# Position maxima taken in front of the turning of the projected tile, in the first attention phase

## The reference

```python
x = x + attn_a(layernorm(x))   # 32 heads of 16, 8 key/value heads, rotary positions, causal softmax
x = x + ffn(layernorm(x))      # 512 -> 1376 -> 512, 4-bit codes with scales plus a rank-32 correction
x = x + attn_b(layernorm(x))   # 32 heads of 16, biases, causal softmax
x = x + ffn(layernorm(x))
```

## Time and profile before

| | us |
|---|---|
| median of 3 runs | 1864.1 |
| lowest, highest | 1847.99, 1868.69 |
| the profiled execution, device time | 1864.23 |
| its span in the trace | 1862.1 |

### The profile page before, as it was taken

How to read it: one execution, slowest core, us unless ns; L and a number is a source line. 1 busy time by engine, 2 the same in 40 slices (tenths; PEclk the granted TensorE clock), 3 DMA queues, 4 the chain that set the end, 5 groups by cost and what they waited for, 6 DMA issues and landing times. The chain is left out here.

```text
span 1862.1 us, 31544 instructions
## 1 busy us (share of the span) xinstructions
PE 1663.4 (89%) x10736; PEld 1159.2 (62%) x10736; DVE 1098.9 (59%) x2401; ACT 862.2 (46%) x1537; POOL 594.1 (32%) x1542
## 2 busy tenths in 40 slices
PE   5888989989987999999678899889899878999997
PEld 4555655655645777877555566566466456777785
DVE  6777677676663845545455655655654638464543
ACT  4556555555552545435334443443444435454441
POOL 3445344444340312213124333333433312131211
PEclk9999999999997999999889899999899899999999
DMA  2000100100114410112333533433453335201010
GB/s 103 2 25 14 36 24 13 36 25 14 36 36 137 152 68 1 68 38 70 110 51 47 80 59 69 75 54 69 69 70 64 52 112 179 79 23 68 0 45 23
DMA packets 78117, 106.95 MB, mean 57 GB/s; under 512 B 13194, under 2 KB 49674, under 8 KB 77972
## 3 DMA queue, kind: packets, MB, share of 16 engines
q1 hardware_dynamic: 77972, 105.10, 23.4%
HBM read 62.34 MB, written 16.78 MB: 42 GB/s over the span
## 5 line engine op out<-in xcount | busy, mean ns | idle before, releaser
L1495 POOL TENSOR_TENSOR f_ht<-f_work,f_ht 128x512 fp32r<-128x512 f32 (+1 forms) x88 | 114.5, 1305 | 513.6 <-ACT f_ht L1553 513.6
L921 ACT ACTIVATE aa_region<-aa_scores 128x512 f32<-128x512 f32 x320 | 184.7, 599 | 84.0 <-PE aa_scores L1215 80.9
L921 ACT ACTIVATE ab_region<-ab_scores 128x512 f32<-128x512 f32 x320 | 181.2, 601 | 73.4 <-PE ab_scores L1215 72.8
L1638 DVE TENSOR_TENSOR f_work<-f_ring,f_work 128x512 f32<-128x512 f32 (+1 forms) x176 | 120.4, 689 | 133.9 <-ACT f_work L1542 111.8
L1542 ACT ACTIVATE f_work<-f_ring,f_scales 128x512 f32<-128x512 f32 (+1 forms) x176 | 120.3, 685 | 165.8 <-PE f_ring L295 165.4
L295 PE MATMUL f_ring<-xt,f_up_codes 128*128 128x512 f32 (+1 forms) x704 | 180.1, 398 | 8.9 <-DVE f_work L1638 4.5
L295 PE MATMUL f_ring<-f_dcodes,f_ht 128*128 128x512 f32 (+1 forms) x704 | 174.5, 402 | 9.9 <-DVE f_down_x L1607 9.4
L295 PE MATMUL f_ring<-xt,f_gate_codes 128*128 128x512 f32 (+1 forms) x704 | 181.7, 401 | 0.0
L774 POOL TENSOR_SCALAR_AFFINE_SELECT ab_region<-ab_region 128x256 f32<-128x256 f32 (+1 forms) x320 | 115.1, 366 | 182.7 <-ACT ab_region L921 182.1
L1175 PE MATMUL ab_maxima<-ab_stacks 96*128 96x128 bf16 (+3 forms) x512 | 143.7, 318 | 25.1 <-DMA ab_stacks<-ab_parted 13.6
L1175 PE MATMUL aa_maxima<-aa_stacks 96*128 96x128 bf16 (+3 forms) x512 | 142.9, 313 | 25.5 <-DVE aa_nmax L1035 17.7
(11 more groups left out here) (190 smaller groups left out, 3067.2 us busy)
## 6 DMA issues: line engine op xcount, KB each, us to landing
ab_stacks<-ab_parted SPq DMA_DIRECT2D x192, 128.0 KB, 4.2
f_raw<-mid SPq DMA_DIRECT2D x32, 256.0 KB, 4.5
f_x<-mid SPq DMA_DIRECT2D x28, 256.0 KB, 4.2
f_raw<-in_gate_q SPq DMA_DIRECT2D x10, 512.0 KB, 5.4
f_raw<-in_up_q SPq DMA_DIRECT2D x10, 512.0 KB, 4.2
f_raw<-in_down_q SPq DMA_DIRECT2D x10, 512.0 KB, 3.9
aa_x<-in_x SPq DMA_DIRECT2D x18, 256.0 KB, 2.9
ab_x<-mid SPq DMA_DIRECT2D x18, 256.0 KB, 3.1
```

Source lines behind the costliest of these rows:

```text
L921: act.activation(probs[:, s // 2 % 2, SUB * (s % 2) + i, :], scores[:, sbk, :], ACT.Exp, scale=0.25).then_inc(scores_freed[sbk].sem, 1)
L1495: pool.tensor_tensor(ht[0:r, LO, n, :], hid[0:r, n % 2, :], ht[0:r, HI, n, :].bitcast(F32), ALU.subtract).then_inc(hid_lo.sem, 1)
L1638: dve.tensor_tensor(dst, src, scaled[0:r, j, :], ALU.add)\
```

## The change

In VectorE's list the call of `maxima_of` for the position moves from behind the loop over the P tasks to in front of it. Nothing is added or removed, no buffer or semaphore changes, and no other engine's stream is touched.

```diff
                         dve.tensor_tensor(rest[:], src, parted[:, a, 0, :], ALU.subtract)\
                            .then_inc(banks.is_free(where, (kind, u, 0, 0)), 1)
+                    if step is not None:
+                        maxima_of(region, b, s, i)
                     for _, bb, u, t in table.started(region, pos, 1, "P"):
 
                         dve.wait_ge(v_hi.sem, v_hi.at(b0 + bb, u * NT + t + 1))
...
                             rotate(where, b0 + bb, u, t)
                         else:
                             remainder(where, b0 + bb, u, t)
-                    if step is not None:
-                        maxima_of(region, b, s, i)
                     tokens_of(region, pos, b0)
                     if rope:
                         for _, bb, u, t in table.started(region, pos, 2, "P"):
```

## The result

The changed kernel took 1870.72 us as the median of 19 runs, the kernel before 1861.61 us over 19; the ratio is 1.0047 with a 95% interval of 1.0034 to 1.006. That is 8.7 us (6.3 to 11.2) slower; 9.2 us were forecast (1873.4, counted from 1864.2). A second series of the same kernel gave 1.0047 again.

A forecast was written before the change was run, and what follows sets the result against it. TensorE was taken to bound the kernel, busy 89% of the span. Place terms, 4 x (0.27 + 0.51 + 0.27 + 0.34) + 3 x (0.27 + 0.40 + 0.27 + 0.27) = 9.2 us, took 1864.2 to 1873.4; range 1858 to 1885.

The forecast's parts named there:

- Can the idle time be filled?: VectorE's wait before the rotation: no, the maxima block completes 0.24 us after the rotation could start, 0.03 with block 2.
- What moves: Block 0 or 1: rotation, task bank and `roped` 0.81 us later, maxima buffer 1.19 earlier, VectorE's work behind 0.27 later.
- P at 9: Projection at position 9, four places: late bank delays the second T part, then the next; +0.51 us each, the worst.
- P at 49: Projection at position 49, three places: as at 9, but two VectorE waits swallow the bank's delay; +0.40 us each.
- P at 4: Projection at position 4, four places: bank costs nothing, VectorE's unbroken run before block 5 starts later; +0.27 us each.
- I leave it out of the sum: Late `roped` holds ScalarE's copy and one exponential; up to 0.1 us more at P at 9, elsewhere under other waits.
- P at 15: Projection at position 15, four places: the T part's delay disappears in the next wait, for VectorE's F finish; +0.27 us each.
- P at 21: Projection at position 21, block 2, four places: T part 0.53 us later, block 5's 0.19 wait goes; +0.34 each.
- The sum: All 28 places: 5.6 + 3.6 = 9.2 us slower, 1873.4 us, +0.5%.
- P at 55: Projection at position 55, three places: as at 15, with a 0.2 us wait on block 5; +0.27 us each.
- The clock: New stops bring 1.2 GHz stretches at some of 8 places, 1.41 us per fall; at most 1884.7 us; chance 0.12.
- Buffers come free earlier, and that wins: Rival: TensorE's waits on maxima shrink at 28 places, -15.1 us, 1849.1 us, faster by 0.8%; chance 0.05.

The follow-up runs named there:

- the two kernels with the idle instruction: Kernel before plus one unread VectorE sum of constant tiles at 28 places, in front of the rotation (ratio 1.007) or behind its sum (1.0075).
- block 2 alone: Kernel before with the maxima moved in front of the rotation only at the four places with maxima block 2; ratio 1.000.
- late bank: Kernel before, but at 24 places the task bank is freed by the first reduction behind the rotation, 0.72 us later; ratio 0.9993.
- statistics first: Kernel before, with the statistics of a coming x tile taken in front of the rotation behind P at 44, three places; ratio 0.9957.

## Why the prediction was right, point by point

- **Can the idle time be filled? No.** Right. The block is complete 0.24 to 0.27 us behind the v copy at the places with block 0 or 1. The kernel in which TensorE makes it earlier gets back four fifths of the loss in the distances 9 to 15, 15 to 21 and 55 to 60, but only a third of it in 60 to 4 and half in 4 to 9.
- **What moves.** Right: the T part that takes the bank starts 2.16 us after the projection's end instead of 1.36, 0.80 later (forecast 0.81), the list 0.27. That the list is paid one for one was argued; the two kernels with the idle instruction show it (0.41 us at 28 places, 13 and 14 us).
- **P at 9, +0.51: too much, measured 0.28.** The step that failed is the readiness of the next T part. It was taken as its start less the idle time of its row, 188.67 - 0.30. The idle time counts from the modelled end of the matmul in front; the rows show the next one starting before such an end (190.38 behind 190.27 + 0.27). In the profile after the T part follows its predecessor by 192.48 - 191.29 = 1.19 us without a wait, not 1.35. With 1.19 the walk gives 187.83 + 1.19 = 189.02, +0.35, and the part does start 0.34 us later (3.35 us behind the projection's end, 3.01 before). Behind P at 49 the same reading made 0.40 of 0.21. The late bank is even less than that: alone it costs some 0.1.
- **P at 4, 15, 21 and 55: too little, by 0.10 to 0.20.** Three steps failed. The first is "I leave it out of the sum", of `roped`. Behind P at 4 it is the chain over ScalarE, which the forecast set to nothing: the remainder L1020 waits for the high part, and that for the sum.

```profile
182.44 0.32 DVE L1001 TENSOR_TENSOR aa_turned<-aa_tasks,aa_trig 128x160 f32<-128x160 f32 x1
...
184.01 0.46 ACT L931 CAST aa_staged<-aa_rest 128x320 bf16<-128x320 f32 x1 [1.29 <-DVE aa_rest L1007]
...
184.50 0.49 DVE L1020 TENSOR_TENSOR aa_rest<-aa_rest,aa_staged 128x320 f32<-128x320 f32 x1
...
185.02 0.39 PE L1215 MATMUL aa_scores<-aa_stacks 99*128 99x256 bf16 x2 [1.06 <-ACT aa_region L921]
```

  It runs 184.50 - 182.44 = 2.06 us after the rotation's start, at once behind ScalarE's copy (184.01 + 0.46), and VectorE, which would have been ready 0.1 us before, lost that. Also, TensorE here waits 1.06 us for the exponential held behind that copy; it lies under the wait that follows, as forecast. The second was not seen at all: behind P at 15 and 55 the sum itself became 0.10 us longer, as a mask of GpSimd was still running when it started (last section).

  The third is the 0.19 us that the forecast gives back behind P at 21, "and that goes": it was the wait of a weight load, and the product behind it hardly gained. The changed kernel (the projection ends at 214.30), and below it the one row of the kernel before (210.16) that the earlier trace rows does not show:

```profile
216.59 0.65 PE L1328 MATMUL aa_tasks<-identb,aa_staged 128*96 128x128 bf16 x8 [0.69 <-DVE aa_turned L1003]
...
217.58 0.38 PE L1175 MATMUL aa_maxima<-aa_stacks 96*128 96x512 bf16 x1
```

```profile
212.92 0.39 PE L1175 MATMUL aa_maxima<-aa_stacks 96*128 96x512 bf16 x1
```

  The T part waits 0.69 us for the bank instead of 0.16 and starts 0.52 later, counted from the projection's end; block 5 stands at 3.28 instead of 2.76, still 0.52 later. So here it is the late bank that TensorE pays, some 0.5 us at each of four places, while VectorE's list loses next to nothing. Two other kernels show the same distance 21 to 44: the one with the change at block 2 alone has 38.74 us, and the one of the last section, whose sums are not lengthened, 38.69 and 38.74.
- **The sum.** 9.2 forecast, 8.7 measured, 9.8 by the distances. Measured less forecast, -0.9 us for P at 9 and -0.6 for P at 49 stand against +0.4 for each of P at 4 and 15, +0.8 for P at 21 and +0.3 for P at 55. That they nearly cancel is luck; the total is better than its terms. As the rows now have it, 24 x 0.27 of list, 4 x 0.5 of the bank behind P at 21, 4 x 0.1 of the chain behind P at 4 and 0.6 of lengthened sums are 9.5 us.
- **The clock.** Partly right as a mechanism, and no part of the sum. One of the signs by which the prediction would be wrong did appear: the projection of P at 9 ran at half clock in three of four batches, where before it did in none:

```profile
455.63 0.39 PE L1215 MATMUL aa_scores<-aa_stacks 99*128 99x256 bf16 x2 [1.06 <-ACT aa_region L921]
...
457.13 0.39 PE L1175 MATMUL aa_maxima<-aa_stacks 96*128 96x512 bf16 x1 [0.83 <-DVE aa_nmax L1035]
...
457.39 3.89 PE L295 MATMUL aa_tasks<-aa_w,xt 128*128 128x384 f32 x12
```

  The projection took 3.89 us instead of 2.35, behind waits of 1.06 and 0.83 us where there was one of 1.28. These falls belong to the change: 4 to 9 holds one in 8 of 12 batches of the two profiles of the changed kernel and of the one with late masks, and in 1 of 16 of the four kernels whose order at this place is the old one (before, late bank, block 2 alone, statistics first). The Trainium skill's rule that activity releases the full clock (TensorE: Matmul & The Clock Gate, What's actually happening) fits these rows. But the same profile has lost two stretches in which the kernel before fell (60 to 4 took 33.96 and 33.94 us there and 31.01 here), so the first matmul of the feed-forward ring starts at 583.0 us in the changed kernel's profile and at 584.1 in that before. The second profile of the changed kernel falls at 4 to 9 in two batches and not in three. Over the runs the two sides about cancel: the mean granted clock was 0.955 in the 10 and 19 runs of the changed kernel and 0.954 in the 24 of the kernel before, so the slowdown is not lost clock. Such falls come and go by 1.4 us and more, and hide a change of 9 us in a single profile.
- **Buffers come free earlier, and that wins.** Did not happen: TensorE's idle time in front of the maxima products fell from 23.6 us to 19.0 (a fall of over 5 was named as a sign of being wrong), but those in front of T parts (+6.4), scores (+4.6) and F (+2.3) grew by more. Only kernels that shorten VectorE's list or fill its waits won.

## What to carry to other kernels

When an engine works through a fixed list, ask of a move what its list behind the moved part loses or gains, before asking what is released earlier: here 0.27 us of list at 24 places, 6.5 us, was most of the cost, and a bank released 0.7 us late at those places cost almost nothing. At the other four, where TensorE was already waiting for the bank, its delay of 0.5 us was paid in full. So look too for the places where the waiting engine already waits for what the move makes later. Before moving work into an engine's idle time, compare to a tenth of a microsecond when that work's input is complete; work that needs nothing of the awaited producer (the statistics) is what fits there. A saving of the order of 0.5% on this kernel is read from distances between recurring events in the trace, at equal clock, and not from a profile's span.

## What the runs showed that was not expected

**VectorE and GpSimd hold each other.** VectorE's sum of 128x320 takes 0.49 us alone and longer when a mask of GpSimd is still running as it starts. The timeline of the changed kernel behind P at 15:

```profile
204.55 0.41 POOL L774 TENSOR_SCALAR_AFFINE_SELECT aa_region<-aa_region 128x256 f32<-128x256 f32 x1 [0.66 <-ACT aa_region L921]
204.71 0.59 DVE L1007 TENSOR_TENSOR aa_rest<-aa_turned 128x320 f32<-128x320 f32 x1
```

The 7 sums behind P at 15 and 55 took 0.59 us and the 4 behind P at 21 0.66, with a mask of 256 columns ending 0.25 and 0.32 us into them (as above, 204.55 + 0.41 - 204.71); behind P at 9, where it ends 0.14 us in, the sum took 0.49. In the kernel before only one of 28 took over 0.52. It works the other way too: the mask of 128 columns, 0.29 us alone, took 0.44 where it began 0.20 us into a sum, in the kernel before:

```profile
179.58 0.49 DVE L1007 TENSOR_TENSOR aa_rest<-aa_turned 128x320 f32<-128x320 f32 x1
179.78 0.44 POOL L774 TENSOR_SCALAR_AFFINE_SELECT aa_region<-aa_region 128x128 f32<-128x128 f32 x1 [0.21 <-ACT aa_region L921]
```

The Trainium skill (SBUF — State Buffer, SBUF: two separate sides) has the rule: the two engines share a pair of ports as an exclusive lock, which a VectorE instruction with two SBUF inputs and a GpSimd instruction that reads SBUF hold for their whole duration, and the second waits. The rows agree in who waits, but not in how long: overlaps of 0.25 and 0.32 us cost 0.10 and 0.17, some 0.15 less than the whole, and one of 0.14 costs nothing. One more kernel tests it:

```diff
                         bs, s, i = step
+                        if rope:
+                            for _, bb, u, t in table.started(region, pos, 1, "P"):
+                                pool.wait_ge(roped.sem, roped.at(b0 + bb, u * NT + t + 1))
                         causal(b0 + bs, s, i)
```

> The changed kernel, and GpSimd gives its causal mask at the position of a rotation only when VectorE's sum of that rotation is made (28 places). It tests why 11 of the 28 sums took 0.59 or 0.66 us: if a mask of GpSimd that is still running when the sum starts holds it, all 28 sums now take 0.49 us, and the distances 15 to 21 and 55 to 60 are 11.63 and 8.31 us instead of 11.73 and 8.41, 21 to 44 is 0.17 shorter; 1.4 us in all, not to be told from 0 by the time. If the longer sums have another cause (the columns, TensorE's or ScalarE's access), they stay at 0.59 and 0.66. The masks come up to 1 us later, and may hold the next tasks of GpSimd.

All 28 sums took 0.49 us; the groups by line from 56 to 495 us (busy us, mean ns, idle before) of this kernel, where the sum stands at L1010:

```profile
L1010 DVE TENSOR_TENSOR aa_rest<-aa_turned 128x320 f32<-128x320 f32 x28 | 13.8, 492 | 1.0
```

and of the changed kernel:

```profile
L1007 DVE TENSOR_TENSOR aa_rest<-aa_turned 128x320 f32<-128x320 f32 x28 | 15.2, 541 | 1.0
```

The distance 15 to 21 is 11.65 us and 55 to 60 8.33, against 11.73 and 8.41 in the changed kernel and the expected 11.63 and 8.31. But 21 to 44 is not 0.17 shorter, as expected: 38.74 and 38.69 us, against 38.75 and 38.86 in one profile of the changed kernel and 38.74 and 38.72 in the other. There the longer sum holds nobody. The time, 1.0053 (1.0026 to 1.0081), is that of the changed kernel; it can't tell a gain of this size from none. So the sums are lengthened by 7 x 0.10 + 4 x 0.17 = 1.4 us, and 7 x 0.08 = 0.6 us of it is part of the loss, a second-order effect of moving the rotation onto a mask.

**VectorE waits 0.12 us for itself** where an instruction reads what the one before wrote. Filling that with the maxima, which are ready, took 0.1 us off four of the eight distances in the trace (1.8 us in all); the 6.7 us of the runs are more than that shows.
